# Rotary tables on ScalarE's DMA queue, the key rotated ahead of later weight splits, and GpSimd's part of wo in pieces of 512 columns

## What is computed

```
x  = x + attention(layernorm(x), ctx)          # x, ctx: (8, 128, 256)
x  = x + moe(layernorm(x))

attention: q = rope(rms(xn @ wq) * q_norm_w)   # 16 heads of 128, wq (256, 2048)
           k = concat(rms(ctx @ wk_ctx) * k_norm_w, rope(rms(xn @ wk) * k_norm_w))   # 4 kv heads
           v = concat(ctx @ wv_ctx, xn @ wv)
           p = softmax(q k^T / sqrt(128) + causal mask on the second half)   # 256 keys
           out = (p v) @ wo                    # wo (2048, 256)
moe:       8 experts of width 128, the best 2 of each token, and one shared expert
```

## Time and profile before

| | |
|---|---|
| time before, median of 3 executions (lowest, highest) | 361.87 us (359.09, 362.88) |
| the profiled execution: its own time, its span | 362.58 us, 360.8 us |
| PE busy | 327.0 us (91%) |
| DVE busy | 314.5 us (87%) |
| ACT busy | 259.9 us (72%) |
| POOL busy | 166.7 us (46%) |
| mean granted TensorE clock | 0.982 of full |
| chain that ended last: PE, DVE, ACT, issue, POOL, DMA | 40%, 19%, 19%, 11%, 6%, 2% |

### The profile page before, as it was taken

The page is one execution under the profiler, slowest core; times in us unless marked ns, Lnnn a source line. Parts: engine busy times, 40 slices in busy tenths (PEclk is TensorE's granted clock), DMA queues, the critical chain, the costliest instruction groups (busy, mean ns, idle before and its releaser), DMA issues.

```text
span 360.8 us, 7355 instructions
## 1 busy us (share of the span) xinstructions
PE 327.0 (91%) x2250; PEld 219.6 (61%) x2254; DVE 314.5 (87%) x602; ACT 259.9 (72%) x910; POOL 166.7 (46%) x241
## 2 busy tenths in 40 slices
PE   6677869779999999999999999999999999999994
PEld 5253635447665856585667566756766587856452
DVE  1578999989999899999998999899989997875773
ACT  4577769666898599759974997498759875747541
POOL 4366465854375427443734443454436431054530
PEclk9998989989999999999999999999999999999998
DMA  5996300002007100710031001000000000044683
GB/s 172 344 287 226 54 0 0 3 0 45 0 1 174 44 0 0 182 36 1 0 73 29 0 0 29 15 0 0 15 15 0 3 2 0 2 83 94 132 162 115
DMA packets 42450, 21.07 MB, mean 58 GB/s; under 512 B 31672, under 2 KB 39872, under 8 KB 42432
## 3 DMA queue, kind: packets, MB, share of 16 engines
q1 hardware_dynamic: 42432, 20.86, 22.7%
HBM read 12.20 MB, written 1.05 MB: 37 GB/s over the span
## 4 chain that ended last, share of the span: by engine, by line
PE 40%; DVE 19%; ACT 19%; issue 11%; POOL 6%; DMA 2%; SPq 1%; DVEq 1%; ACTq 0%; POOLq 0%
PE proj L1388 10%; ACT probs L566 8%; PE pt_ps L1351 6%; DVE probs L1003 4%; PE o_ps L1361 4%; PE proj L1203 4%; PE turn L1297 4%; POOL q_rot L795 3%; DVE nmax L991 3%; PE sc_ps L1318 3%; DVE pT_lo L929 2%; ACT pT_hi L471 2%; DMA wq<-in_L_xattn_wq_dram 2%; ACT kc_junk L510 2%; ACT q_junk L510 2%
## 5 line engine op out<-in xcount | busy, mean ns | idle before, releaser
L566 ACT ACTIVATE probs<-sc_ps,nbias,q_r 128x256 f32<-128x256 f32 x128 | 71.0, 574 | 6.5 <-DVE nbias L995 6.0
L795 POOL TENSOR_TENSOR q_rot<-q_t 128x512 f32<-128x512 f32 x32 | 42.4, 1325 | 42.6 <-DVE q_t L922 41.8
L1003 DVE TENSOR_SCALAR probs<-probs,rden 128x256 f32<-128x256 f32 x128 | 51.0, 460 | 1.1
L510 ACT ACTIVATE q_junk<-proj 128x128 bf16<-128x128 f32 x128 | 34.3, 304 | 12.9 <-DVE q_t L922 12.9
L1203 PE MATMUL proj<-wq_hi,xT 128*128 128x512 f16 x128 | 39.0, 387 | 3.8 <-DVE wq_lo L913 3.4
L471 ACT ACTIVATE pT_hi<-pt_ps 128x512 f16<-128x512 f32 x64 | 34.8, 598 | 9.2 <-PE pt_ps L1351 9.2
L929 DVE SCALAR_TENSOR_TENSOR pT_lo<-pt_ps,pT_hi 128x512 f16<-128x512 f32 x64 | 40.9, 680 | 0.2 <-ACT pT_hi L471 0.2
L991 DVE TENSOR_REDUCE nmax<-sc_ps 128x4 f32<-128x1024 f32 x32 | 38.9, 1214 | 1.5 <-PE sc_ps L1340 1.5
L749 POOL TENSOR_TENSOR q_r<-q_me,power 128x4 f32<-128x4 f32 x32 | 34.5, 1077 | 2.5
L1351 PE MATMUL pt_ps<-ident,probs 128*128 128x128 f32 x256 | 33.3, 273 | 0.4 <-DVE probs L1003 0.3
L471 ACT ACTIVATE qT_hi<-turn 128x512 f16<-128x512 f32 x32 | 19.6, 613 | 18.2 <-PE turn L1297 18.2
(11 more groups left out here) (216 smaller groups left out, 866.2 us busy)
## 6 DMA issues: line engine op xcount, KB each, us to landing
wq<-in_L_xattn_wq_dram SPq DMA_DIRECT2D x4, 512.0 KB, 9.1
w<-in_L_ffn_w_dram SPq DMA_DIRECT2D x2, 1024.0 KB, 10.4
wq<-in_L_xattn_wo_dram SPq DMA_DIRECT2D x1, 2048.0 KB, 8.1
ctx_b<-in_ctx_dram SPq DMA_DIRECT2D x8, 128.0 KB, 2.3
out_dram<-x_all SPq DMA_DIRECT2D x4, 256.0 KB, 2.2
x_all<-in_x_dram SPq DMA_DIRECT2D x1, 896.0 KB, 12.4
wkc<-in_L_xattn_wk_ctx_dram SPq DMA_DIRECT2D x1, 512.0 KB, 4.4
wk<-in_L_xattn_wk_dram SPq DMA_DIRECT2D x1, 512.0 KB, 5.3
```

The lines of the kernel that those rows point to most:

```text
L510: last = nc.scalar.activation(junk[:, head], bank[:, head], ACT.Square, scale=scale, accum_out=dst[:, h:h + 1])
L566: last = nc.scalar.activation(probs[:, h, :], sc_ps[:, h, :], ACT.Exp, bias=nbias[:, h:h + 1], scale=q_r[:, g, h:h + 1], accum_out=den[:, ...
L795: nc.gpsimd.tensor_tensor(q_rot[:], q_t1[:], q_t2[:], ALU.add).then_inc(q_added, 1)
L1003: last = nc.vector.tensor_scalar(probs[:, h, :], probs[:, h, :], rden[:, h:h + 1], None, ALU.mult)
```

## The change

* The three tables that the key needs (`kw_sb`, `cos_sb`, `sin_sb`) are started from ScalarE's queue as soon as row 0 of x has landed, and signal `d_tab_k`. `qw_sb` (signal `d_tab_q`) and `kw_col` are started there after `ln_high(0)`. SyncE's list has wq's group 0 next after wk; behind it SyncE waits for `wkc` before it starts group 1. wv_ctx and wv go behind group 2.
* GpSimd makes the key's tables and the query's tables each on its own signal, and VectorE waits for the key's alone ahead of `k_turn(0)`.
* `wc_split(0)` moves: on ScalarE from ahead of `kc_squares(0)` to behind `q_copy(0, 0)`, on VectorE from ahead of `k_turn(0)` to behind `q_turn(0, 1)`. On ScalarE `k_squares(0)` stands ahead of `kc_scale(0)`.
* GpSimd's part of wo is done in pieces of 512 columns: two scalings in row 0 at g = 1, two at g = 2; two low halves in row 0 at g = 3, two in row 1 at g = 0.
* One `keep_warm(16)` becomes `keep_warm(4)`.

```diff
         d_wo = sem("d_wo")
-        d_tab = sem("d_tab")
+        d_tab_k = sem("d_tab_k")
+        d_tab_q = sem("d_tab_q")
         d_kw = sem("d_kw")
...
         quarter_heads = H // 4
-        own_wo = slice(2 * quarter_heads, H)
+        own_wo = [slice(h, h + H // 8) for h in range(2 * quarter_heads, H, H // 8)]
...
             sp.dma_start(wk32[:], parts(wk)).then_inc(d_wk, 16)
-            sp.dma_start(cos_sb[:], cos).then_inc(d_tab, 16)
-            sp.dma_start(sin_sb[:], sin_signed).then_inc(d_tab, 16)
-            sp.dma_start(qw_sb[:], q_norm_w.partition_broadcast(P)).then_inc(d_tab, 16)
-            sp.dma_start(kw_sb[:], k_norm_w.partition_broadcast(P)).then_inc(d_tab, 16)
-            sp.dma_start(kw_col[:], k_norm_w.unsqueeze(1)).then_inc(d_kw, 16)
             for g in range(G):
...
                 sp.dma_start(wq32[:, :, cols], parts(wq)[:, :, cols]).then_inc(d_wq[g], 16)
-                if g == 1:
+                if g == 0:
+                    sp.wait_ge(d_wkc, 16)
+                if g == 2:
                     sp.dma_start(wvc[:], parts(wv_ctx)).then_inc(d_wvc, 16)
...
             copy(warm[:], scale_x[:])
+            act.wait_ge(d_x0, 16)
+            act.dma_start(kw_sb[:], k_norm_w.partition_broadcast(P)).then_inc(d_tab_k, 16)
+            act.dma_start(cos_sb[:], cos).then_inc(d_tab_k, 16)
+            act.dma_start(sin_sb[:], sin_signed).then_inc(d_tab_k, 16)
...
             def wo_split(i):
-                act.wait_ge(*((d_wo, 16) if i < 2 else (wo_scaled, 1)))
+                act.wait_ge(*((d_wo, 16) if i < 2 else (wo_scaled, 2 * i - 2)))
                 heads = slice(i * quarter_heads, (i + 1) * quarter_heads)
...
             ln_high(0)
+            act.dma_start(qw_sb[:], q_norm_w.partition_broadcast(P)).then_inc(d_tab_q, 16)
+            act.dma_start(kw_col[:], k_norm_w.unsqueeze(1)).then_inc(d_kw, 16)
             in_copies(0)
...
             split_high(wq32[:, :, 0:GW], wq_hi[:, :, 0:GW])
-            wc_split(0)
             kc_squares(0)
...
             copy(kw_scaled[:], kw_col[:], K_SCALE).then_inc(c_kw, 1)
+            k_squares(0)
             kc_scale(0)
-            k_squares(0)
             act.wait_ge(c_kw, 1)
...
             q_copy(0, 0)
+            wc_split(0)
             act.wait_ge(d_wq[3], 16)
...
+            def wo_rest(half):
+                pool.wait_ge(wo_high, 3 + half)
+                for heads in own_wo[2 * half:2 * half + 2]:
+                    nc.gpsimd.tensor_tensor(wo_lo[:, heads, :], wo32[:, heads, :], wo_hi[:, heads, :],
+                                            ALU.subtract).then_inc(wo_low2, 1)
+
             ln_root(0)
...
-            pool.wait_ge(d_tab, 64)
             HW = P // 2
-            for w, c, s in ((kw_sb, k_cos, k_sin), (qw_sb, q_cos, q_sin)):
+            for w, c, s, loaded, count in ((kw_sb, k_cos, k_sin, d_tab_k, 48), (qw_sb, q_cos, q_sin, d_tab_q, 16)):
+                pool.wait_ge(loaded, count)
                 nc.gpsimd.tensor_tensor(c[:], cos_sb[:], w[:], ALU.mult)
...
                         q_roots(b + 1, 0)
-                    if first and g == 1:
+                    if first and g in (1, 2):
                         pool.wait_ge(d_wo, 16)
-                        nc.gpsimd.tensor_tensor(wo32[:, own_wo, :], wo32[:, own_wo, :],
-                                                scale_w[:].unsqueeze(2).broadcast_to([P, H // 2, D]),
-                                                ALU.mult).then_inc(wo_scaled, 1)
+                        for heads in own_wo[2 * g - 2:2 * g]:
+                            nc.gpsimd.tensor_tensor(wo32[:, heads, :], wo32[:, heads, :],
+                                                    scale_w[:].unsqueeze(2).broadcast_to([P, H // 8, D]),
+                                                    ALU.mult).then_inc(wo_scaled, 1)
                     if first and g == 3:
-                        pool.wait_ge(wo_high, 4)
-                        nc.gpsimd.tensor_tensor(wo_lo[:, own_wo, :], wo32[:, own_wo, :], wo_hi[:, own_wo, :],
-                                                ALU.subtract).then_inc(wo_low2, 1)
+                        wo_rest(0)
+                    if not first and isinstance(b, int) and b == 1 and g == 0:
+                        wo_rest(1)
                     if cast:
...
             split_low(wq32[:, :, 0:GW], wq_hi[:, :, 0:GW], wq_lo[:, :, 0:GW], 2)
-            wc_split(0)
-            dve.wait_ge(c_tab, 2)
+            dve.wait_ge(c_tab, 1)
             k_turn(0)
...
             split_low(wq32[:, :, GW:2 * GW], wq_hi[:, :, GW:2 * GW], wq_lo[:, :, GW:2 * GW], 3)
+            dve.wait_ge(c_tab, 2)
             q_turn(0, 0)
...
             q_turn(0, 1)
+            wc_split(0)
             split_low(wq32[:, :, 3 * GW:4 * GW], wq_hi[:, :, 3 * GW:4 * GW], wq_lo[:, :, 3 * GW:4 * GW], 5)
...
                 if g == 0:
-                    pe.wait_ge(wo_low2, 1)
+                    pe.wait_ge(wo_low2, 4)
                     pe.wait_ge(wo_low, 2)
...
                 pe.wait_ge(q_sq, G * b + G + 3)
-                pe.wait_ge(wo_low2, 1)
+                pe.wait_ge(wo_low2, 4)
                 pe.wait_ge(wo_low, 2)
...
             q(0, 1)
-            keep_warm(16)
+            keep_warm(4)
             k_turn(0)
...
             q_turn(0, 0)
```

## The result

The changed kernel takes **354.41 us** (median of 6 runs, 354.17 to 355.51). The kernel before takes 361.48 in the same comparison (6 runs, 359.09 to 362.88). The ratio is 0.9843, interval 0.9803 to 0.9882: 7.07 us less, where 7.9 were forecast. The profiled execution of after, the longest of its six, took 355.51 us, with a span of 353.8 and a mean granted clock of 0.999. Before: 362.58, 360.8, 0.982.

What follows compares the result with a forecast made beforehand. Loop rows were taken as full on TensorE and VectorE, so gains lay ahead of the first output projection at 82.84 us. Terms summed to -7.9 us, from the median of 361.87 to 354.0 us, range 350.8 to 358.7.

Steps and rivals of the forecast that it cites:

- k_turn(0): VectorE's step on row 0's key: starts at 11.9 in place of 16.22 us, -4.3 us.
- the wait for v: VectorE's 1.01 us wait for v after L848's bias, put down to TensorE's late start: vanishes, -1.0 us.
- pieces 3 and 4: GpSimd's wo pieces at g = 2, ahead of q_add(1, 1), push it into the probabilities' division: +1.1 us (0 to 2).
- wo_rest(1): Two GpSimd pieces behind ln_rs, awaited by the first output projection, may hold VectorE up once: +0.4 us (0 to 1.5).
- Loads, wq0 at 9.4: wq's first group, started at 2.74 us, lands at 9.4; wq1 lands by 11, needed about 11.6, so covered.
- wk_ctx put back: VectorE's wk_ctx split between q_turn(0, 1) and wq3's split, plus a lock wait for wq3's low half: +2.3 us.
- VectorE's waits gone: VectorE's waits for TensorE's q(0, 2) and v vanish: -1.6 us; a falling clock would cost 0.9 of it.
- L843: GpSimd wo instruction of 4.26 us; in pieces, the bias takes 0.2 for 1.71: -1.5; the wait after: -0.5 us.
- L848: GpSimd wo instruction of 4.05 us; in pieces, the bias takes 0.4 in place of 3.16: -2.8 us.
- queues only interleave: Rival: table descriptors still take turns between wq's; wq0 gains 2.4 us, lands at 10.4; 354.8 us, chance 0.14.
- The lock as often as before: Rival: wo pieces still block VectorE, so L843, L848 and waits behind give nothing: 358.7 us, chance 0.16.
- more than forecast: Rival: wq3's split isn't held up, pieces 3 and 4 meet nothing, the clock stays: 351.8 us, chance 0.10.

Runs made afterwards that it cites:

- e3: The changed kernel without SyncE's wait for wkc ahead of wq's group 1: 354.63 us, ratio 0.9814.
- e6: The changed kernel without q_norm_w's load, the query's tables made from k_norm_w: 354.55 us.
- a0: The changed kernel itself, run again unaltered on the same chip as other runs: 354.40 us, ratio 0.9804.
- e8: The changed kernel with all five table loads on SyncE behind wq0, no load started from ScalarE, no SyncE wait: 354.92 us, ratio 0.9827.
- e4: The changed kernel with both halves of the wk_ctx split back in their old places, ahead of k_turn(0) on VectorE: 354.35 us, ratio 0.9835.
- e7: e5 with ScalarE's squares of q(0, 0) moved ahead of the high half of wq2's split: 352.15 us, ratio 0.9743.
- e1: The changed kernel with GpSimd's part of wo whole again, loads and moved splits kept: 358.65 us, ratio 0.9941.
- e2: The kernel before with only GpSimd's part of wo cut into pieces: 355.62 us, ratio 0.9867.
- e5: The changed kernel with the wk_ctx split in idle time, behind q_turn(0, 0) on VectorE and kc_squares(0) on ScalarE: 353.58 us, ratio 0.9809.

## Why the prediction was right, and where its steps were off

The time is right (354.0 forecast, 354.41 measured), the first projection stands at 74.92 (forecast 75), the rows at 35.08 (35.1). That the sum meets the projection to the tenth is partly luck: `k_turn(0)` gave 0.7 less than forecast and the wait for v 0.5 less, and pieces 3 and 4 and `wo_rest(1)` cost 0.3 and 0.7 less. The terms:

- *Loads, wq0 at 9.4*: its split starts at 9.35, directly behind that of wk, so it had landed by then. *"Lands by 11 and is needed at about 11.6. That is covered"*: wrong. wq1 was there at 13.21, because SyncE started it at 6.10, behind the small loads, and the stretch with empty engines lay behind wq0. In e3, started ahead of them, its split stands at 11.35. It cost some 0.4 us at nmax (0, 0) in this execution (27.40 against 26.96 in e6), and 0.1 or nothing where wq1 came at 12.7 (a0), so the error stayed nearly hidden. The reason given for the gain, that small loads ahead of wq hold it back, fits e8, where wq0 goes first in the one queue. That they need a queue of their own falls.
- *Starts on ScalarE, nothing*: right, 0.33 to 0.74 us each, inside the idle time.
- *k_turn(0), -4.3*: mis-sized, -3.6 (-3.9 in `a0_changed_again`). The sum had GpSimd's three tables at 1.1 us. They took 2.98, from 9.58 to 12.56, since VectorE's splits of wk and wq0 lie beside them. The lock was counted only from the rotation on; VectorE waited 0.49 for the tables, and its own split of wq0 took 1.48 where the like takes 1.22.
- *wk_ctx put back, +2.3*: right in size and kind (+2.3 between `k_turn(0)` and nmax (0, 0), the wq3 split at 2.29 us). e4 takes it out and stands 2.05 earlier at the projection.
- *VectorE's waits gone, -1.6*: -1.6 by nmax (0, 2). Its condition was sized wrong. It said that v costs 0.9 if the clock falls again. The clock fell in the profiled executions of e3 and e8, which have the change's order, and cost nothing: the stretch to nmax (0, 1) took 8.64 as in after. It fell in e7's, where VectorE is some 3 us further ahead, and cost 1.7, all of the term.
- *L843, -1.5 and the wait behind it, -0.5*: -1.6 and -0.6. *Pieces 3 and 4, +1.1*: +0.8. *L848, -2.8*: -2.8. *The wait for v, -1.0*: only -0.5, and its reason, TensorE's late start behind the bias, is wrong: e1 has the bias of 3.16 and no wait for v, with the clock at 1.00. *wo_rest(1), +0.4*: nothing of it is seen; the projection gained another 0.3. Together -5.0 in the trace, with -4.3 forecast and -4.9 by e2.
- *The 12 warm products less*: not run by themselves. The clock stays at 1.00 throughout after's front.
- *The median*: the sum was made against an execution of 362.58, 1.1 us above the median of its six, and taken from the median. After's profiled execution lies 1.1 us above its own median, so the two profiled ones differ by the same 7.07. What is missing from 7.9 is lost behind the first projection, some 0.9 us: 0.16 by the next row, and 0.7 behind row 7's projection (67.6 us before, 68.3 after). It is 67.9 in the profiled execution of `a0_changed_again`, the same kernel, and what makes it differ stays open.

The rivals: *queues only interleave* had wq0 at 10.4 and the gain at 2.4; its split started at 9.35, 3.5 us ahead of before's, and at 8.82 in e8 from one queue, so the tables don't hold it back once it goes first. *The lock as often as before* falls with the biases at 0.16 and 0.39. *ScalarE stops at its starts* falls with rows of 0.33 to 0.74. Of *more than forecast* only the clock came: wq3's split was held up (2.29 us), and pieces 3 and 4 met the division (1.94).

## What to carry to other kernels

Look at instructions that took longer than their like, not only at idle time: two biases of four columns, at 1.71 and 3.16 us behind GpSimd instructions of 4.26 and 4.05, were the larger part of this change (e2: 4.9 us), and cutting those two instructions into four pieces each, half of them one group later, was all it needed. A step moved off a wait lands somewhere else: give it a place where its engine is idle and the lock is free (e5), not merely a later one. Before giving transfers a queue of their own, try their order in the one queue; and where TensorE idles for about 2 us, and the clock falls behind it in one execution and not in another, go by all executions and not by one trace.

## What the runs showed of the hardware that I had not expected

- A load of one 512-byte row to 128 partitions left the DMA engines at a share of 0.26 to 0.52 for 2 us while a 512 KB load of the other queue was under way. Leaving it out gave 0.82 to 1.00 (e6), and so did starting that load and the one behind it ahead of the small one (e3: 0.84 to 0.94 from 8.5 to 10.0). Its kind alone isn't enough either: k_norm_w's load, which e6 keeps, has the same form. What sets it off stays open.
- Turns at the lock touch small instructions the most: 128 columns took 1.45 us on GpSimd, 64 columns 1.30 against 0.31. The Trainium skill, SBUF — State Buffer, on its two separate sides, has the pair as an exclusive lock for a whole instruction. The rows agree, and show besides that who waits gets the next turn: at 24 us two splits and `q_rot` alternate, and each behind the first waits once, 0.9 and 1.1 us.
- The same kernel (e4) took 352.8 to 353.5 us with the clock at 0.998 or 0.999, and 355.2 to 355.6 with it at 0.987 to 0.989: 2 us that a single trace doesn't show. In before TensorE idled 1.96 us, from 28.04 to 30.00, ahead of one low stretch. In after it idles 1.96 us too, from 24.49 to 26.45, and the clock stays. In e3 it idles the same 1.96 us, and the clock falls to 0.50 from 28 to 30.
